# Reordering the expert-choice feed-forward stage: score turning, first selection round, shared-expert down projections and the last expert pair

## The reference, cut to what matters

```python
e = 16; cap = int(s * 2.0 / e)                       # 128 tokens
logits = jnp.einsum('bsd,ed->bse', hidden_states, gate_w)
scores = jax.nn.softmax(logits, axis=-1).transpose(0, 2, 1)
topk_w, topk_idx = jax.lax.top_k(scores, cap)
x_tok = jnp.take_along_axis(hidden_states[:, None, :, :], topk_idx[..., None], axis=2)
g = jnp.einsum('becd,efd->becf', x_tok, Wg)          # f = 512
u = jnp.einsum('becd,efd->becf', x_tok, Wu)
h = jax.nn.gelu(g, approximate=False) * u
eo = jnp.einsum('becf,edf->becd', h, Wd) * topk_w[..., None]
flat = flat.at[flat_idx].add(eo.reshape(-1, d))      # scatter back
shared = einsum(gelu(hidden_states @ Ws_g.T) * (hidden_states @ Ws_u.T), Ws_d)
return out + shared                                  # x = x + tanh(g_ffn[0]) * this
```

## Time and profile before

| | us |
|---|---|
| median of 3 runs (lowest, highest) | 1088.47 (1084.37, 1095.37) |
| the profiled execution, its own time | 1089.12 |
| span of its instructions | 1087.4 |
| mean granted TensorE clock in it, share of full | 0.957 |

### The profile page before, as it was taken

The page is one execution under the profiler, slowest core; times in us unless marked ns, Lnnn a source line. Parts: engine busy times, 40 slices in busy tenths (PEclk is TensorE's granted clock), DMA queues, the critical chain, the costliest instruction groups (busy, mean ns, idle before and its releaser), DMA issues. The chain is left out here.

```text
span 1087.4 us, 17908 instructions
## 1 busy us (share of the span) xinstructions
PE 971.9 (89%) x6268; PEld 823.9 (76%) x6269; DVE 612.7 (56%) x1273; ACT 488.4 (45%) x732; POOL 275.2 (25%) x260
## 2 busy tenths in 40 slices
PE   5899989969999999867788889889998899999994
PEld 3687878858888888555667668767786799999994
DVE  5686849971222311689798899857685522222221
ACT  2544431211111111578676687364452456565650
POOL 3000000031454442261005211200000244444442
PEclk8899999989999999889999899989998899999998
DMA  5600031014675753102000010036114333333331
GB/s 141 202 12 20 20 102 56 20 57 127 171 202 171 215 167 66 41 1 78 1 1 2 1 39 1 2 110 231 40 40 145 93 49 48 48 48 48 48 44 20
DMA packets 67813, 79.65 MB, mean 73 GB/s; under 512 B 12656, under 2 KB 52171, under 8 KB 67755
## 3 DMA queue, kind: packets, MB, share of 16 engines
q1 hardware_dynamic: 54123, 60.27, 16.9%
q0 software_dynamic: 13632, 18.62, 10.1%
HBM read 60.73 MB, written 17.83 MB: 72 GB/s over the span
## 5 line engine op out<-in xcount | busy, mean ns | idle before, releaser
L2923 PEld LDWEIGHTS ps<-room,xn_sb 128*128 128x128 f32 x1248 | 145.5, 192 | 2.8 <-issue 0.8
L2923 PE MATMUL ps<-room,xn_sb 128*128 128x128 f32 x1248 | 146.2, 275 | 0.6 <-issue 0.6
L269 POOL TENSOR_TENSOR norm_vec<-norm_vec,powers 128x4 f32<-128x4 f32 (+3 forms) x27 | 28.8, 1067 | 372.3 <-DVE norm_vec L263 371.4
L2628 DVE TENSOR_TENSOR room<-room,ps 128x1024 f32<-128x1024 f32 x24 | 29.3, 1220 | 112.3 <-PE ps L2269 59.1
L2990 ACT ACTIVATE xn_sb<-w_L_ffn_w 128x1024 f32 x78 | 82.2, 1058 | 21.1 <-DVE f_te L3087 11.1
L2876 POOL DMA_INDIRECT out_x<-f_yo,f_give x39 | 61.9, 1588 | 111.3 <-DVE f_yo L3119 108.4
L3113 DVE TENSOR_TENSOR room<-room,ps 128x512 f32<-128x512 f32 x39 | 26.8, 687 | 111.3 <-PE ps L2923 111.3
L2278 PE MATMUL ps<-b_room,room 128*128 128x256 f32 x384 | 85.0, 379 | 0.0
L2278 PEld LDWEIGHTS ps<-b_room,room 128*128 128x128 f32 x384 | 72.9, 190 | 9.9
L2238 POOL DMA_INDIRECT acc_rows<-f_eo,f_idx x32 | 52.4, 1637 | 101.8 <-DVE f_eo L2657 54.2
L2451 ACT ACTIVATE room<-ps 128x1024 f32<-128x1024 f32 x24 | 24.6, 1024 | 118.8 <-PE ps L2261 118.8
(11 more groups left out here) (384 smaller groups left out, 2053.4 us busy)
## 6 DMA issues: line engine op xcount, KB each, us to landing
w_L_ffn_w<-in_L_ffn_w SPq DMA_DIRECT2D x24, 512.0 KB, 9.0
b_room<-in_L_ffn_Wg SPq DMA_DIRECT2D x16, 512.0 KB, 4.7
b_room<-in_L_ffn_Wu SPq DMA_DIRECT2D x16, 512.0 KB, 6.2
b_room<-in_L_ffn_Wd SPq DMA_DIRECT2D x16, 512.0 KB, 5.5
xn_rows<-xn_sb SPq DMA_DIRECT2D x8, 512.0 KB, 2.9
x_sb<-in_x SPq DMA_DIRECT2D x4, 512.0 KB, 6.9
xn_sb<-in_L_ffn_w SPq DMA_DIRECT2D x2, 1024.0 KB, 7.6
x_sb<-acc_rows SPq DMA_DIRECT2D x4, 512.0 KB, 5.4
```

What stands on the lines that cost most here:

```text
L2628: dve.tensor_tensor(hT[p][:, :, :].rearrange("p a c -> p (a c)"), ge[p][:, :], ps[:, 2:4, :].rearrange("p a c -> p (a c)"), ALU.mult).then ...
L2923: m = pe.matmul(ps[:, banks[p], f * P:(f + 1) * P], wb[p][:, n, i, f * P:(f + 1) * P], xsT[p][:, i * P:(i + 1) * P], start=(i == 0), stop= ...
```

## The change

On PE, the scores are turned after half of the gate projection of unit 0 (`up_gate_part`). The down projections of units 4 and 5 no longer follow their value projections: that of unit 4 stands after the context work, ahead of the turning of `tf` and `tw`, that of unit 5 behind it. In the first pair of experts the gate projection of the first comes before the second one's rows are turned. In the last pair, taken out of the loop, the first down projection comes before the second value projection. On DVE, the copy of the scores is gone: the first round reads them in PSUM, and PE's next work on those banks waits for `rnd` at 2 instead of 1. `hidden` of unit 5 moves behind `wcol`, and in the last pair the first result is weighed ahead of the second `hidden`. ACT and POOL get the two late units' work in the matching places: on ACT behind the context work, on POOL behind the first four gather instructions.

```diff
-    STEPS_BEFORE = [2, 4, 10, 5, 10, 4]
+    STEPS_BEFORE = [5, 4, 10, 5, 10]
...
-                for u in range(FIRST):
+                for u in range(FIRST - 2):
+                    add_x(u)
                 pool.wait_ge(i_rdy, 1)
                 pool.wait_ge(ahead.rows_out, ahead.n_out)
                 gather(0)
                 gather(1)
+                add_x(FIRST - 2)
+                add_x(FIRST - 1)
...
-                up_gate(pe, 0, sg, unit(0))
+                up_gate_part(pe, 0, sg, unit(0), range(0, 2))
                 pe.wait_ge(sc_rdy, 1)
...
                 m.then_inc(v_ps, 1)
+                up_gate_part(pe, 0, sg, unit(0), range(2, FT)).then_inc(g_ps, 1)
                 up_value(pe, 0, su, unit(0))
...
-                    for p in range(2):
-                        down(pe, u + p, p, sd)
-                pe.wait_ge(rnd, 1)
+                    if u + 2 < FIRST:
+                        for p in range(2):
+                            down(pe, u + p, p, sd)
+                pe.wait_ge(rnd, 2)
                 nxt.keys_tensor(pe)
...
                 side.context_tensor(pe, (ge_sb, FIRST + 1))
+                down(pe, FIRST - 2, 0, sd)
                 pe.wait_ge(t_rdy, 1)
...
+                down(pe, FIRST - 1, 1, sd)
                 pe.wait_ge(i_rdy, 2)
...
+                turn_tokens(0, 0)
+                gate_of(0, 0)
+                turn_tokens(0, 1)
+                value_of(0, 0)
+                gate_of(0, 1)
+                value_of(0, 1)
+                down_of(0, 0)
+                down_of(0, 1)
...
-                with pe.Fori(1, E // 2) as pair:
+                with pe.Fori(1, E // 2 - 1) as pair:
                     two_experts(pair)
+                last = E // 2 - 1
+                turn_tokens(last, 0)
+                turn_tokens(last, 1)
+                gate_of(last, 0)
+                value_of(last, 0)
+                gate_of(last, 1)
+                down_of(last, 0)
+                value_of(last, 1)
+                down_of(last, 1)
...
+                for p in range(2):
+                    gelu(FIRST - 2 + p, p)
                 nxt.keys_scalar(act)
                 act.wait_ge(cleared, 1)
                 side.context_scalar(act)
+                for p in range(2):
+                    shared_out(FIRST // 2 - 1, p)
...
-                then(dve.tensor_copy(va[0][:, :], ps[0:B * E, 6:8, :].rearrange("p a c -> p (a c)")))
-                dve.sem_inc(rnd, 1)
...
+                    left = va[r % 2][:, :] if r else ps[0:B * E, 6:8, :].rearrange("p a c -> p (a c)")
...
-                        then(dve.match_replace(va[1 - r % 2][:, :], best, va[r % 2][:, :], -1.0))
+                        then(dve.match_replace(va[1 - r % 2][:, :], best, left, -1.0))
+                        if r == 0:
+                            dve.sem_inc(rnd, 1)
...
+                hidden(FIRST - 1, 1)
                 bit.sums(dve)
...
+                    hidden(e + FIRST, 0)
+                    if e == E - 2:
+                        weighed(e, 0)
+                    hidden(e + 1 + FIRST, 1)
```

More of the change, by code:

```diff
@@ L2214, in _, with add_x @@
                 bit.constants(pool)
-                for u in range(FIRST):
+                def add_x(u):
                     pool.wait_ge(y_sb, u + 3)
@@ L2255, in _, with up_gate_part @@
                 side.first_rows(pool)
-            def up_gate(pe, n, g, rhs):
+            def up_gate_part(pe, n, g, rhs, parts):
                 pe.wait_ge(ge_sb, n + 1)
-                for f in range(FT):
+                for f in parts:
                     for k in range(KT):
@@ L2262, in up_gate @@
                                       start=(k == 0), stop=(k == KT - 1))
-                m.then_inc(g_ps, 1)
+                return m
+            def up_gate(pe, n, g, rhs):
+                up_gate_part(pe, n, g, rhs, range(FT)).then_inc(g_ps, 1)
             def up_value(pe, n, u, rhs):
@@ L2314, in _, with turn_tokens @@
                 pe.transpose(ps[:, 6, 128:128 + B * E], tw[:, :], K.ident[0:B * E, 0:B * E]).then_inc(t_ps, 1)
+                down(pe, FIRST - 1, 1, sd)
                 pe.wait_ge(i_rdy, 2)
+                def turn_tokens(pair, p):
+                    pe.wait_ge(gat[p], 32 * pair + 32)
+                    pe.wait_ge(xt_sb, 2 * pair + p + 1)
+                    for k in range(KT):
+                        for b in range(B):
+                            m = pe.transpose(ps[:, 6 + p, (k * B + b) * P:(k * B + b + 1) * P],
+                                             xg[p][:, b, k * P:(k + 1) * P], K.ident[:, :])
+                    m.then_inc(xt_ps, 1)
@@ new lines, in tokens, with gate_of, value_of, down_of @@
+                def tokens(p):
+                    return [xgT[p][:, k, :] for k in range(KT)]
+                def gate_of(pair, p):
+                    pe.wait_ge(xt_sb, 2 * pair + p + 3)
+                    pe.wait_ge(w_in[p], 32 * pair + 32)
+                    up_gate(pe, 2 * pair + p + FIRST, buf.wg[p], tokens(p))
+                def value_of(pair, p):
+                    up_value(pe, 2 * pair + p + FIRST, buf.wu[p], tokens(p))
+                def down_of(pair, p):
+                    pe.wait_ge(d_in[p], 16 * pair + 16)
+                    down(pe, 2 * pair + p + FIRST, p, buf.wd[p])
@@ L2317, in two_experts @@
                 def two_experts(pair):
-                    e = 2 * pair
+                    turn_tokens(pair, 0)
+                    turn_tokens(pair, 1)
                     for p in range(2):
[L2320 to L2326, removed]
@@ L2457, in _, with shared_out @@
                 act.activation(lg[:, :, :], lg[:, :, :], ACT.Exp).then_inc(exp_done, 1)
-                with act.Fori(0, FIRST // 2) as pair:
-                    u = 2 * pair
+                def shared_out(pair, p):
+                    act.wait_ge(y_ps, 2 * pair + p + 3)
+                    act.wait_ge(out_dma[p], 32 * pair + 32)
+                    act.activation(eo[p][:, :, :].rearrange("p a c -> p (a c)"), ps[:, 4 + p, :],
+                                   ACT.Copy, scale=gate).then_inc(y_sb, 1)
+                with act.Fori(0, FIRST // 2 - 1) as pair:
                     for p in range(2):
-                        gelu(u + p, p)
+                        gelu(2 * pair + p, p)
                     for p in range(2):
[L2463 to L2466, removed]
+                        shared_out(pair, p)
+                for p in range(2):
+                    gelu(FIRST - 2 + p, p)
                 nxt.keys_scalar(act)
@@ L2631, in _ @@
                 step = 0
-                for u in range(FIRST):
+                for u in range(FIRST - 1):
                     for _ in range(STEPS_BEFORE[u]):
```

36 lines of the change are left out of this document (20 added, 16 removed).

## The result

The changed kernel took 1079.39 us in the median of 17 runs (1077.03 to 1085.54), the kernel before 1085.84 in 17 runs beside them. The ratio is 0.9952 with a 95% interval of 0.9935 to 0.9968: 5.2 us gained, between 3.5 and 7.1 (the two medians by themselves are 6.45 apart). So the fair comparison is that of the gains: 7.5 forecast, 5.2 timed, and 7.3 between the two profiled executions (span 1087.4 and 1080.1).

What follows compares the result with a forecast made beforehand. PE, busy 89% of the span, bounds the kernel; time is won only where it stands still or runs at half clock. Gains 6.9 + 0.6 = 7.5 us, from the 1088.47 median to 1081.0; range 1075.5 to 1086.5 (8 in 10).

Steps and rivals of the forecast that it cites:

- The scores' part: Stage start: scores turned earlier without the copy; first `max` 3.2 us earlier, places 4.5 earlier, PE then late by 1.4.
- The down projections and the gathers: From the keys to the first pair's end: keys 6.9 us earlier, first gather 3.45 earlier, pair's end 6.9 earlier.
- The cross check by kinds: PE up to the first pair's end: 10.4 us of idle and cold work go, waits of 0.7, 1.8, 0.9 come: 7.0.
- First and last pair: Expert pairs reordered: 0.5 us of turning moves inside the first; the last gains 0.6 at ACT's start on the rows.
- Rival A: PE's new waits between 225 and 236 us cost the clock: 2.46 or 4.9 us more, 1083.5 to 1086; 13%.
- Rival B: At the stage's start, turning the scores delays the clock's rise: 1.2 to 3.7 us, 1082.2 to 1084.7; 10%.
- C: Last pair loses: scatter or read back goes no earlier, PE's 1.5 us stands alone, 1083.1; 8%.
- D: Slower than before: clock falls before unit 4's down projection, 64 instructions at half clock, 9.9 us, 1090.9; 3%.
- E: More than forecast: clock holds after the stage, 2.2 to 3.5 us come back, 1077.5 to 1078.8; 12%.
- F: Selection gets no earlier, through PSUM reads or a late `hidden`: 2.3 us lost for the reads, 1083.3; 4%.

Runs made afterwards that it cites:

- e1: Kernel before with only the scores' part: scores turned after half of the first gate projection, first round read from PSUM; ratio 0.9988.
- e2: Changed kernel with the scores' part undone (turned behind the whole gate projection, copied to SBUF, old steps); ratio 0.9974.
- e5: Kernel before with ten matmuls, unused by the result, put into PE's wait for the first gather; ratio to the kernel before 0.9992.
- e6: Changed kernel with unit 5's product on DVE ahead of the last eight selection steps, not behind the indices; ratio to the kernel before 0.9943.
- e3: Changed kernel with the first pair of experts in the old order, both turnings first; ratio to the kernel before 0.9972.
- e4: Changed kernel with the last pair of experts in the old order, in the loop; ratio to the kernel before 0.9934.
- e8: e7 with ACT copying the first expert's turned rows ahead of scaling unit 5's result; ratio to the kernel before 0.9877.
- e12: Kernel before, unchanged, run and profiled again; median 1086.66 us, ratio 1.0009.
- e10: Changed kernel, unaltered, run and profiled again; ratio to the kernel before 0.9959.
- e9: e8 with the first half of unit 4's down projection moved up between the keys and the context; ratio to the kernel before 0.9899.
- e7: Changed kernel with half of unit 4's down projection ahead of the turning of the indices, half behind it; ratio to the kernel before 0.9923.
- e11: e8, unaltered, run and profiled again; ratio to the kernel before 0.9907.

## Why the prediction was right, point by point

The steps of the sum, counted from S:

| step | forecast | measured |
|---|---|---|
| first `max` | 4.3 | 4.35 |
| keys begin | 57.9 | 57.77 |
| places ready on DVE | 70.1 | 69.28 |
| indices turned | 71.5 | 71.59 |
| first gather | 72.3 | 72.43 |
| first gate projection | 78.6 | 78.45 |
| first pair's end | 100.0 | 99.88 |
| read back issued | 265.2 | 265.07 |
| next rows on ACT | 273.8 | 273.70 |

**The scores' part.** Right, and for the reason given: as PE is late and not DVE, nothing of it is needed until the down projections move (e1), and then it is worth 1.5 us (e2). DVE was ready 0.8 sooner than forecast: before, it had waited 0.57 and 0.20 for value projections and 0.32 ahead of unit 5's product, and none of these is left; PE was late by 2.3 instead of 1.4. It has no effect.

**The down projections and the gathers.** Right to 0.2 us at each step. The cross check by kinds (4 us of waiting, 3 of clock) agrees with e5, which takes the clock's part alone. e6 shows that the wait of 1.57 is not one to remove by itself: the gathered rows are the next thing that is late, by 1.2 us.

**First and last pair.** In the traces 0.85 (e3) and 0.75 (e4, forecast 0.6); no time on record resolves either.

**Rival A** (the clock falls in the new waits) did not come in the two profiles of the changed kernel nor in e3 and e4, which have the same wait for the product. It came in two relatives whose waits are a little different, at 1.6 us (e2) and 1.7 (e6); in e8 the clock fell ahead of these waits, in the context work, for 1.6. The mechanism is real, its price was set too high: 2.46 is for 16 instructions wholly at half clock, and it was half for a part of them. How often it comes in the changed kernel is open. **Rival B** (the clock rises late) did not come: about S+3 in both. The Trainium skill (TensorE: Matmul & The Clock Gate, Part 4: PE-mode transpose) would have had the turned scores hold it up. In e8 the scores were turned wholly at half clock, and right behind the turning the clock came back (0.73 from 161 to 162). The stretch at half clock, 158.1 to 161.5, was no longer than that of the changed kernel (156.4 to 159.8), in which only projections ran from S on; that rule isn't borne out here. **C** is out by e4. **D** did not come. **E** did not: the clock falls behind the stage in both profiles of the changed kernel (0.84 and 0.92 over the 22 us from 8 us behind ACT's start). But the fall that E wanted to save is not in every execution of the kernel before. The same 22 us in its two profiles, the first one and e12, PE alone:

```profile
446.52:468.52 22.00, 16.20 (x58) 0.84 0.00 0
...
446.61:468.61 22.00, 15.56 (x68) 1.00 0.00 0
```

**F** is out by the rows on `max`.

**The size.** The traces have 7.6 and 7.7 us in the stage in the two pairs of profiles, the times have 5.2 (3.5 to 7.1) and, in e10, 0.9959, that is 4.5 (1.4 to 7.5). Some 2 us of the traced gain don't arrive on average, and that is the term that the prediction didn't have. The granted clock shows where to look. Count what the clock falls short of 1.00 in a window, times its length, as us of full clock. From S to the end of the first pair, in windows of 2 us, it is 6.7 and 6.8 in the profiles of the kernel before and 1.5 and 1.7 in those of the changed one, 5.1 less. The mean clock of the whole program is on record for every execution from e1 on and for the changed kernel's 17: 0.9575 over 103 executions of the kernel before, 0.9601 over 28 of the changed one, which makes 46.1 and 43.0 us, only 3.1 less (1.2 to 4.9). So about 2 us of clock (0.2 to 3.9) that the stage gives in the profiles are missing in the whole. That has the right size, though a wait at half clock counts in these sums too and costs no time by its clock.

Where they are lost is not shown. Behind the stage I cut the 640 us from ACT's start on the next rows into 15 windows and took the same sum: 29.4 and 27.9 us in the two profiles of the kernel before, 31.0 and 31.6 in those of the changed one, 2.6 more on average, in code that the change doesn't touch (in slices of 10 us up to the end, 33.3 and 28.6 against 35.3 and 34.9); "rest" is 648.9 and 642.4 against 649.6 and 649.4. But over the twelve experiments the sum of the 15 windows goes from 23.1 (e9, "rest" 641.4) to 36.3 (e1, 651.3) with no order in it that I can read. One window lost in both pairs, the 60 us from 290 us behind ACT's start (0.97 to 0.95, and 1.00 to 0.97), and in slices of 5 us the falls in it lie at different places. So with two profiles of each it is argued, not shown. The other candidate is rival A in some executions of the changed kernel: at 1.6 us a time it would have to come in all of them to make 2 us, and it came in neither profile, so it can be a part at most. The first guess at the place (the kernel before pays less than 6.08 on average) was tested by e12 and not supported. It stays open.

## What to carry to other kernels

Before moving an engine's work forward, write down when each of the producers at a join is ready. The selection on DVE and the context work on PE came within 0.4 us of each other, so that speeding up DVE alone was worth nothing (e1), clearing PE alone brought the indices 1.9 us (e2), and both together 3.4. A wait that is filled can pay twice, here 4 us of waiting and 3 of clock; but what is left of it in short waits can still lose the clock (1.6 and 1.7 us in e2 and e6). And split the filling work where the producer is ready: the whole block of 3.5 us in front of the turning held it up by 1.8 us against half of it (e7).

## What the runs showed of the hardware

The clock fell in stretches in which PE never stood still for more than 1.6 us: in e2 with waits of 1.34 and 1.57, in e8 with PE busy 3.1 of the 4 us around the fall, on short matmuls. In e8 it also fell 1.3 us into a projection that ran without a gap (at 158.1; S is 156.87). In e11, the same kernel as e8, the same context work kept it (1.32 us for the 8 matmuls that took 2.07 in e8). VectorE's `max`, `max_index` and `match_replace` on 32 x 1024 float32 values take 1.2 us each whether they read PSUM or SBUF. And the same unchanged 640 us of this kernel differed by 6.5 us between two executions of one program (648.9 and 642.4; whether they ran on the same chip is not on record), which is why a traced gain in a stage and a timed one should both be given.
